# Four transformer-style layers on one core: the order of the second chunk layer and the full attention

## The reference

```python
def chunk_layer(x, ctx):            # layers 0 and 2; 8 heads of 16, chunks of 64 positions
    q, k, v = projections of ctx    # not of x
    o = softmax(q k / 4) v          # inside each chunk of 64
    return layer_norm((o @ W_out + b_out) * mask + x)
x1 = chunk_layer(x, ctx)
# layer 1: full attention, 128 tokens of width 1024, 32 query and 8 key heads of 32
h  = x1 + attention(q = x1 Wq, k = ctx Wk, v = ctx Wv) Wo      # Wq.. with their LoRA parts folded in
x3 = layer_norm((chunk attention of ctx with its own weights + b_out) * mask + h)
# layer 3: 30 nearest neighbours of the 1024 points, whose coordinates are channels of ctx;
# angles of the neighbours -> small MLP with batch norms -> softmax -> weighted sum of x3
out = x3 + aggregate(x3, neighbours(ctx), attention weights)
```

## Time and profile before

| | |
|---|---|
| time, median of 3 runs (lowest to highest) | 8223.11 us (8183.79 to 8232.78) |
| the profiled execution | 8271.05 us |
| its span, from first to last instruction | 8269.3 us |
| mean granted TensorE clock, as a share of 2.4 GHz | 0.859 |
| busy share of PE, DVE, ACT, POOL | 83%, 75%, 52%, 32% |
| loop of 32 items | about 80 us to 6590 us of the span |

### The profile page before, as it was taken

How to read it: one execution, slowest core, us unless ns; L and a number is a source line. 1 busy time by engine, 2 the same in 40 slices (tenths; PEclk the granted TensorE clock), 3 DMA queues, 4 the chain that set the end, 5 groups by cost and what they waited for, 6 DMA issues and landing times.

```text
span 8269.3 us, 204463 instructions
## 1 busy us (share of the span) xinstructions
PE 6884.4 (83%) x79422; PEld 4925.1 (60%) x79422; DVE 6179.9 (75%) x8508; ACT 4307.4 (52%) x9907; POOL 2685.8 (32%) x3399
## 2 busy tenths in 40 slices
PE   8888888888888888888888888888888759588888
PEld 5555555555555556555555555655555523488888
DVE  5777777777777777777777777777777747777777
ACT  3555555555555555555555555555555404566666
POOL 2333333333333333333333343333333310111111
PEclk9888888888888888888888888888888779899999
DMA  2111111111111111111111111111111130222222
GB/s 99 55 57 57 55 55 55 55 55 55 55 55 58 58 56 55 55 55 55 55 55 55 55 60 59 56 57 55 59 60 56 63 85 11 68 66 67 65 59 61
DMA packets 295563, 482.41 MB, mean 58 GB/s; under 512 B 103250, under 2 KB 216034, under 8 KB 293698
## 3 DMA queue, kind: packets, MB, share of 16 engines
q1 hardware_dynamic: 240205, 372.00, 15.1%
q10 hardware_dynamic: 54133, 94.55, 3.6%
HBM read 393.25 MB, written 73.25 MB: 56 GB/s over the span
## 4 chain that ended last, share of the span: by engine, by line
PE 54%; DVE 16%; ACT 15%; issue 10%; POOL 2%; DMA 1%; ACTq 1%; DVEq 0%; SPq 0%; POOLq 0%
ACT S L1047 6%; PE SCA L842 6%; PE PD L959 5%; PE SCA L811 4%; PE MISC L664 4%; PE SCA L946 3%; DVE m L1353 3%; ACT kexp L1090 3%; PE TP L834 3%; DVE pd L1359 3%; PE SCB L946 2%; PE PD L639 2%; PE SCA L682 2%; PE SCA L786 2%; PE TP L778 2%
## 5 line engine op out<-in xcount | busy, mean ns | idle before, releaser
L1353 DVE MAX8 m<-pd 128x8 f32<-128x1024 f32 x1024 | 1249.3, 1220 | 210.8 <-ACT pd L1016 99.0
L509 POOL TENSOR_TENSOR prod<-prod,hm 128x480 f32<-128x480 f32 x384 | 406.1, 1057 | 2928.8 <-ACT prod L1041 2762.2
L1357 DVE FIND_INDEX8 idx<-m,pd 128x8 uint32<-128x1024 f32 x1024 | 1248.7, 1219 | 9.5 <-issue 9.5
L1359 DVE MATCH_REPLACE8 pd<-m,pd 128x1024 f32<-128x1024 f32 x768 | 929.8, 1211 | 0.0
L639 PE MATMUL PD<-arena 128*128 128x512 f32 x1028 | 660.8, 730 | 149.7 <-ACT pd L1016 127.5
L664 PEld LDWEIGHTS MISC<-ptab,gat 128*128 128x128 bf16 x23400 | 673.8, 99 | 107.1 <-issue 77.7
L1600 DVE TENSOR_TENSOR gat<-maskT,con 120x2048 f32<-120x2048 f32 x256 | 592.1, 2352 | 171.2 <-PE SCA L946 162.3
L664 PE MATMUL MISC<-ptab,gat 128*128 128x24 bf16 x23400 | 667.5, 176 | 35.4 <-DVE gat L1309 20.6
L1047 ACT ACTIVATE S<-SCA,mx 128x64 f32<-128x64 f32 (+1 forms) x2560 | 572.0, 380 | 233.1 <-DVE mx L1365 233.1
L1365 DVE TENSOR_REDUCE mx<-SCA 128x16 f32<-128x1024 f32 (+1 forms) x192 | 235.2, 1225 | 506.9 <-PE SCA L767 456.1
L1047 ACT ACTIVATE S<-SCB,mx 128x64 f32<-128x64 f32 (+1 forms) x2560 | 570.9, 381 | 0.0
(11 more groups left out here) (270 smaller groups left out, 15192.6 us busy)
## 6 DMA issues: line engine op xcount, KB each, us to landing
gat<-low_scratch SPq DMA_DIRECT2D x396, 640.0 KB, 4.2
arena<-in_ctx ACTq DMA_DIRECT2D x33, 512.0 KB, 3.9
maskT<-in_mask ACTq DMA_DIRECT2D x32, 512.0 KB
arena<-in_x ACTq DMA_DIRECT2D x32, 512.0 KB, 6.3
x_scratch<-arena ACTq DMA_DIRECT2D x32, 512.0 KB, 4.8
x3T_scratch<-arena ACTq DMA_DIRECT2D x32, 512.0 KB, 3.7
arena<-x3T_scratch SPq DMA_DIRECT2D x32, 512.0 KB, 7.0
arena<-x_scratch SPq DMA_DIRECT2D x32, 512.0 KB, 9.3
```

The costliest lines, as they stand in the source:

```text
L1353: step(V.max(m, buf[:, :]))
L1357: last = V.max_index(idx[:, t, 8 * r:8 * r + 8], m, buf[:, :])
L1359: step(V.match_replace(buf[:, :], m, buf[:, :], -3.0e38))
```

## The change

The second chunk layer (now s = 1; the full attention is s = 2) runs between the first chunk layer and the full attention. Its output is masked and then added to X1, and `Wo`'s result is added to that sum, so the item ends with `Wo`. X1's transposes go into hT at the start of the second chunk layer's groups, and `query_pair(g)` makes two of the eight column blocks of the full attention's queries in PD in each of these groups. Layer norm 1 and the stores of an item's X0 and table move into the next item: the transposes of X0 become two halves in PD in groups 0 and 1, and the result goes to hT's place, from where it is stored. The chunk layers' output projections go to TP instead of SC[0]. The next item's context is loaded once more, into hT's place, for its squares. `split`, the ctxT transposes, `sides`, `tangents`, `roots`, `divide`, the distances, the rounds and the norms are put elsewhere in the order. K of the full attention is kept in `k1_plain` and spread in group 6. Counts of matmuls, exponentials and rounds stay. The core of the diff (sync bookkeeping and repeated forms cut):

```diff
-        ROUNDS_AT = (0, 0, 1, 0) + (1,) * 8
-        DIST_AT = {2: (2, 0), 3: (2, 1), 4: (4, 1), 6: (5, 0), 7: (5, 1), 8: (7, 1)}
-        NORMS_AT = {9: 0, 10: 1, 11: 2}
+        ROUNDS_AT = (1, 1, 1, 1) + (2, 2, 2, 2) + (1, 1, 1, 1)
+        DIST_AT = {2: (2, 0), 3: (2, 1), 4: (4, 1), 6: (5, 0), 7: (5, 1), 8: (6, 1), 9: (7, 0), 10: (7, 1)}
+        LAST_DIST = {0: (3, 0), 1: (6, 0)}
+        X3_AT = {0: 0, 1: 1}
+        NORMS_AT = {10: 0, 11: 1}
...
 # POOL
                 for n in range(4):
                     consume(i, n)
-                tangents(i)
-                for n in range(4, GROUPS - 1):
+                    sides(i, n)
+                consume(i, 4)
+                tangents(i, 0)
+                consume(i, 5)
+                consume(i, 6)
+                tangents(i, 1)
+                for n in range(7, GROUPS - 1):
                     consume(i, n)
...
 # PE, groups
                     scores(0)
                     scores(1)
+                    if s == 0:
+                        pe.wait_ge(v2_evac, i * 4 + 2)
+                        for t in range(NT):
+                            last = nc.tensor.transpose(TP[:, t * P:(t + 1) * P], ctx[:, t * P:(t + 1) * P], ident)
+                        last.then_inc(ctxT_ready, 1)
+                    if s == 1:
+                        pe.wait_ge(v2_evac, i * 4 + 4)
+                        pe.wait_ge(xl_done, i * 2 + 2)
+                        for kc in range(KC):
+                            last = nc.tensor.transpose(TP[:, kc * P:(kc + 1) * P], X1[:, kc * P:(kc + 1) * P], ident)
+                        last.then_inc(hT_ready, 1)
                     for g in range(4):
+                        if n in X3_AT:
+                            x3_half(i, X3_AT[n])
+                        if s == 1:
+                            query_pair(g)
+                        elif n in DIST_AT:
                             distance(i, *DIST_AT[n])
                         pe.wait_ge(exp_done, i * 12 + n + 1)
...
                         fill(i, n, MISC)
+                        if s == 1 and n in DIST_AT:
+                            pe.wait_ge(pair_evac, i * 4 + g + 1)
+                            distance(i, *DIST_AT[n])
                         pe.wait_ge(et_evac, i * 12 + n + 1)
...
+                    outputs(4 * s + 3)
+                    if s in LAST_DIST:
+                        distance(i, *LAST_DIST[s])
+                    else:
+                        norms(i + 1, 2)
...
+                def query_pair(pair):
+                    if pair == 0:
+                        pe.wait_ge(hT_evac, i + 1)
+                    else:
+                        pe.wait_ge(pair_evac, i * 4 + pair)
+                    pe.wait_ge(pd_evac, i * 16 + (9, 10, 10, 11)[pair])
+                    for c in (2 * pair, 2 * pair + 1):
+                        for kc in range(KC):
+                            last = mm(PD[:, c % 2 * P:(c % 2 + 1) * P], Wq[:, kc, c * P:(c + 1) * P],
+                                      hT[:, kc, :], start=(kc == 0), stop=(kc == KC - 1))
+                    last.then_inc(pair_ready, 1)
...
 # PE, end of the trip
                 for h in range(2):
                     for c in range(KC):
                         last = mm(SC[0][:, h * 512:(h + 1) * 512], OT[:, c * P:(c + 1) * P],
                                   Wo[:, c, h * 512:(h + 1) * 512], start=(c == 0), stop=(c == KC - 1))
-                last.then_inc(oproj_ready, 1)
-                chunk_attention(2)
-                for h in range(2):
+                    if h:
+                        last.then_inc(oproj_ready, 1)
+                    else:
+                        pe.wait_ge(ctx_ld, i * 16 + 32)
                     distance(i + 1, 0, h)
...
 # ACT, groups
+                        if s == 1:
+                            act.wait_ge(table_st, i * 16 + 16)
+                            act.wait_ge(hT_ready, i + 1)
+                            A(hT_flat, TP[:, :], ACT.Copy).then_inc(hT_evac, 1)
                         exponentials(0)
                         expand(2)
+                        if s == 0:
+                            A(ctxT[:, :, :].rearrange("p t c -> p (t c)"), TP[:, :], ACT.Copy).then_inc(ctxT_evac, 1)
...
                             A(ET[:, :], SC[g % 2][:, :], ACT.Copy).then_inc(et_evac, 1)
+                            if n in X3_AT:
+                                x3_half(i, X3_AT[n])
+                            if n == 1:
+                                act.dma_start(table_dram[(i + NB - 1) % NB, :, :].rearrange("(t p) r -> p t r", p=P),
+                                              tab).then_inc(table_st, 16)
+                                act.wait_ge(x3_st, i * 16 + 16)
+                                act.dma_start(X0[:, :], x_in[i, :, :]).then_inc(x_ld, 16)
+                            if g == 0 and s == 1:
+                                expand(3)
+                            if s == 1:
+                                query_pair(g)
                             if g < 3:
                                 exponentials(g + 1)
                             pick(n)
+                            if s == 1 and n in DIST_AT:
+                                distance(i, *DIST_AT[n])
...
 # DVE, groups and the trip
                         if g < 3:
-                            front(l, g + 1, keys)
-                        if n + 1 < GROUPS:
-                            onehot(i, n + 1)
-                        for _ in range(ROUNDS_AT[n]):
-                            search_round()
+                            front(s, g + 1, keys)
+                        if 0 < n < GROUPS - 1:
+                            onehot(i, n if n < 2 else n + 1)
+                        search_round()
+                        if n == 0:
+                            onehot(i, 0)
+                        if n == 1:
+                            onehot(i, 2)
                         if g:
                             normalise(n - 1, keys)
+                        for _ in range(ROUNDS_AT[n] - 1):
+                            search_round()
+                        if n == 6:
+                            divide(i)
                     search_round()
-                    normalise(4 * l + 3, keys)
+                    normalise(4 * s + 3, keys)
...
+                front(0, 0, CHUNK)
+                groups(0, CHUNK)
+                masked(0, X1)
+                dve.wait_ge(x_ld, i * 16 + 16)
+                step(V.tensor_tensor(X1[:, :], X1[:, :], X0[:, :], ALU.add))
+                moments(X1)
                 search_round()
+                scaled(0, X1)
                 for _ in range(3):
                     search_round()
+                front(1, 0, CHUNK)
+                groups(1, CHUNK)
+                search_round()
+                masked(1, X0)
+                front(2, 0, P)
+                V.tensor_tensor(X1[:, :], X1[:, :], X0[:, :], ALU.add).then_inc(res_done, 1)
+                groups(2, P)
                 for _ in range(4):
                     search_round()
+                dve.wait_ge(oproj_ready, i * 3 + 3)
+                step(V.tensor_tensor(X0[:, :], SC[0][:, :], X1[:, :], ALU.add))
+                moments(X0)
+                scaled(1, X0)
```

More of the change, by code:

```diff
@@ L425, in relative, with sides @@
                 G_.tensor_copy(own[:, :, :], ctxT[:, :, 0:3]).then_inc(own_saved, 1)
-            def sides(i, last=False):
+            def sides(i, part=None):
                 count = [0]
@@ L569, in _ @@
             relative(NB + 1, last=True)
[L570 removed]
+            sides(NB + 1)
             tangents(NB + 1)
```

383 lines of the change are left out of this document (191 added, 192 removed).

## The result

| | before | changed |
|---|---|---|
| median (lowest to highest), same chip | 8217.03 us (8183.79 to 8232.78) | 8525.31 us (8505.07 to 8533.71) |
| ratio, 95% interval | | 1.0361, 1.0320 to 1.0403 |
| profiled execution | 8271.05 us | 8533.71 us |
| one item, mean of 31 | 203.1 us | 210.8 us |

The change makes the kernel 3.6% slower. The forecast was 8268 us, the range ended at 8450: the time lies outside. Where it went is read from the stages. The table gives them as means over 31 items, from the start of a stage's first TensorE instruction to that of the next (my own reckoning from the trace; the earlier trace rows show one item).

What follows compares the result with a forecast made beforehand. No engine was taken as the bound, but a ring of hand-overs, 203.7 us per item; walked stages of 202.1 plus 3.0 for restarts gave 205.1, x 32 = +45 us: 8268 us on the median's scale, range 7990 to 8450.

Steps and rivals of the forecast that it cites:

- A: From an item's last output projection to the next item's first transposes: 37.2 us to 28.9, gain 8.3 us.
- B: Groups of the first chunk layer: 28.3 us to 32.7, loss 4.4 us, with five search rounds instead of two.
- idle tail: Ends of the two chunk layers' groups, TensorE without work for 4 and 8 us; 1.5 us for each restart.
- C: First output projection's end to the second's start, without `Wo`: 82.7 us to 28.8 + 48.6 = 77.4, gain 5.3 us.
- D: Second output projection to `Wo`'s end: hand-over 4.8 us, full attention's groups 33.3 to 34.9, `Wo` 15.3 to 16.4; loss 7.5.
- cold restarts: Slow TensorE clock after the idle ends of both chunk layers' groups: 1.5 us each, +3.0 us an item.
- walked 202.1: Sum of all stages of one item, against 203.7 us, before 3.0 us for slow-clock restarts.
- rival 1: Clock and waits turn out well, query pairs keep PE at 2.4 GHz: 196.3 us an item, 7986 us; chance 0.33.
- Rival 3: The forecast: the change only moves the waits, 205.1 us an item, +45 us, 8268 us; chance 0.38.
- Rival 2: The end of group 7 decides: eight groups 0.7 us later plus two restarts, 210.7 us an item, 8447 us; chance 0.29.

Runs made afterwards that it cites:

- experiment 3: Changed kernel with idle matmuls at four places (5, 3, 3 and 8; the 8 ahead of group 7's last outputs): ratio 0.9976 to the kernel before, 202.1 us an item.
- experiment 6: Changed kernel with the mask bias ahead of the fourth search round and the first one-hot ahead of group 0's round: ratio 1.0127 to the kernel before, 206.2 us an item.
- experiment 8: Changed kernel with idle matmuls at all four places and the mask bias and first one-hot earlier: ratio 0.9864 to the kernel before, 198.7 us an item.
- experiment 1: Kernel before with one of eight partial products of the full attention's Q projection left in place: ratio 1.0014, 203.1 us an item as before.
- experiment 10: Changed kernel with earlier bias and one-hot, one search round moved into group 8, idle matmuls (5, 3, 3, 4 in group 7): 8078.47 us, ratio 0.9813 to kernel before.
- experiment 5: Changed kernel with 8 idle matmuls ahead of group 7's last outputs alone: ratio 0.9995 to the kernel before, 202.7 us an item.
- experiment 2: Changed kernel with one of eight partial products of each query pair left in place: ratio 0.9988 to the kernel before, item from 210.8 to 201.9 us.
- experiment 7: Changed kernel with 8 idle matmuls in group 7 and the mask bias and first one-hot earlier: ratio 1.0006 to the kernel before, 201.2 us an item.

## Why the prediction was wrong

**A** held: 8.3 us of gain forecast, 8.0 measured.

**B** was the largest miss: 32.7 walked, 36.8 measured. "Fill(0) and behind it scores(2) wait 2 us for DVE" was right, 2.00 us in the trace. The walk then put the steps at the fast clock. From transposes to transposes it had 8.3, 8.5 and 6.8 us, and 9.1 to the projection; the means are 11.2, 9.2, 6.3 and 10.1. So 2.9 of the 4.1 us are in group 0, where the mean granted clock is 0.65, and 1.0 in the idle tail. Idle matmuls alone leave group 0 at 11.0 (experiment 3), the earlier one-hot alone at 10.9 (experiment 6), both together bring it to 8.6 (experiment 8) and B to 33.5; so clock and order are both in it, and in experiment 8 part of the gain is the shorter wait. The last 0.8 us, in groups 1 and 2 of that run, no experiment explains.

**C.** A premise and a number in it failed. "The 16.19 us of PE that the full attention's queries take in this place are gone" is true and worth nothing (experiment 1). The stretch that held them fell from 34.6 us to 28.8, and by the rows it is VectorE's part that got shorter: from the projection's end to VectorE's first reduction there are 31.4 us before and 20.4 now (one item each). The walked 28.8 us came out to 0.1. The groups then took 52.4 us for 48.6. Walked, they are 14.2, 9.5, 10.9 and 14.0 us; the means are 16.5, 8.9, 11.0 and 15.9. So the miss is group 4 (2.3) and the tail (1.9). Group 4 in the changed kernel, then in the item of experiment 10 shown above:

```profile
2088.25 2.08 PE L661 MATMUL PD<-arena 128*128 128x512 f32 x2 [1.76 <-ACT reg L1114]
...
2091.65 1.99 PE L839 MATMUL SCA<-kexp,reg 64*64 64x256 f32 x16
2093.56 1.93 PE L850 MATMUL TP<-reg,ET 128*64 128x34 f32 x32
```

```profile
1961.33 1.12 PE L661 MATMUL PD<-arena 128*128 128x512 f32 x2 [1.76 <-ACT reg L1125]
...
1963.13 1.09 PE L850 MATMUL SCA<-kexp,reg 64*64 64x256 f32 x16
1964.15 1.13 PE L861 MATMUL TP<-reg,ET 128*64 128x34 f32 x32
```

The wait is the same 1.76 us; the steps take twice as long in the first, and the pair behind them 5.04 us instead of 3.84. In the second the whole group takes 12.3 us. The pairs themselves were sized well: 4.05 us each, and the trace has 3.83, 5.04, 3.74 and 3.84. Besides, 82.7 us was one item; the mean is 85.4, so the gain in C was 4.2 us.

**D.** The hand-over, 4.8 us, is exact. The full attention's groups took 35.7 for 34.9, against a mean of 31.6 before and not the 33.3 of the item that I read, and `Wo` 16.7 against 14.7.

**The clock is the term that was mis-sized.** The step that failed is "In A, B and C I used steps at the fast clock", with 3.0 us added for cold restarts, "1.5 us for each" of the two idle tails. The item is not 3.0 but 8.7 us above the walked 202.1. The tails were priced about right where they stand: 1.0 and 1.9 us. Left out were group 0 (2.9) and group 4 (2.3), which have no idle tail just ahead and which the walk had at the fast clock, while the trace grants 0.65 and 0.69 there (the kernel before has 0.64 in its group 0 as well, which a mean over its items would have shown). The remaining 0.6 us are small differences of both signs.

The 8.1 us of experiment 5 are the price of the wait in group 7, but not the size of this miss. 1.5 of them are in the second output projection and 4.3 in the full attention's groups, and the forecast had both at the slow level already: 3.7 us "as now", and 34.9 built on a row of 33.3 at 0.73, one of the slow items of the kernel before (there these groups take 30.1 to 33.7 us). Measured were 3.4 and 35.7.

Its sum has two slips of 0.1 us (its stages give 202.0, A's steps 28.8), which change nothing.

The Trainium skill's rule ("TensorE: Matmul & The Clock Gate", "What's actually happening"), that the throttled state is the default and activity releases it, bears on rival 1, which had the pairs hold the clock up in C. The trace agrees only in part: the clock came back within pair 1, which began slow, but the mean of C's groups is 0.82 in the changed kernel, with the pairs in it.

**The rivals.** Rival 1 (7986 us) fell: the loop's clock is 0.83 in the changed kernel, not over 0.9. Rival 3, the forecast, fell: the waits did not merely move. Rival 2, "the end of group 7 decides", gave 210.7 us an item where 210.8 was measured. Its mechanism was right: groups late by the clock, added ahead of an idle tail. It had 3.0 us for the two restarts and 5.6 for eight groups running 0.7 us late each; measured are 2.9 in the tails and 5.2 in groups 0 and 4 alone, next to nothing in the others. That the sums agree to 0.1 us is luck, and its sign of a loop clock under 0.8 did not come. Its time for the execution, 8447, was too low even so, because it was carried to the median from a profiled execution 0.6% above it: 32 x 7.7 = 246 us of the 262.7 us between the profiled executions lie in the loop, but the medians are 308 us apart. The 45 us between 262.7 and 308 are that the profiled execution of before lay 54 us above its median, that of the changed kernel 8 above its own.

**What stays open.** The query pairs' 8.9 us (experiment 2) and the tail's 8.1 us (experiment 5) are not two parts of one sum, since the loss is 7.7: fewer products also change when TensorE reaches the tail, and the clock. Their overlap was not measured by itself. Nor was any other part of the change (the halves of X0's transposes, the moved `sides`, `tangents` and loads) taken back alone.

## What to carry to other kernels

Work that an engine does while another sets the pace is free, and moving it is no gain; here 16.19 us of TensorE came from such a place and went to one where they cost 8.9. Look who is busy for nearly the whole of the stretch it leaves and of the one it enters. Price a new TensorE wait by the matmuls of the next 40 us, not by the next three steps, and ask of every group in a walk at which clock it starts. Read a stage as a mean over items: the one item read here was 2 to 3 us off in two stages. Put VectorE's long jobs behind the small result for which TensorE stands. Where such a wait must stay, matmuls that nobody reads can be worth having, if they end before the wait does.

## What the runs showed of the hardware

A single wait of 8.10 us in an item of 210 cost about as much again as it lasted: filled with 7.03 us of unread matmuls, and so made no shorter, it gave 8.1 us back in matmuls at the 2.4 GHz level instead of the 1.2 one. But the wait alone does not settle the clock: in one item of the changed kernel the groups behind the same 8.10 us ran at 1.00 and took 28.67 us, where they took 36.01 at 0.76 in another. And a shorter wait is not enough: in experiment 7 TensorE needed 10.14 us at a granted clock of 0.52 for what took 5.86 us at 1.00. Two groups with the same wait of 1.76 us inside (changed kernel and experiment 10) ran their steps at one level and at the other, 1.99 and 1.09 us for the same scores.
